# Cross-attention by units of eight heads: four key buffers, pairs of score tiles, values in runs, score maxima ahead across units

## What is computed

```python
q = (layernorm(x) @ w_q.T).reshape(8, 56, 16, 8)
k = (ctx @ w_k.T).reshape(8, 1500, 16, 8)
v = (ctx @ w_v.T).reshape(8, 1500, 16, 8)
attn = softmax(einsum('bqhd,bkhd->bhqk', q, k) * 8 ** -0.5, axis=-1)
x = x + tanh(g_xattn) * (einsum('bhqk,bkhd->bqhd', attn, v).reshape(8, 56, 128) @ w_o.T)
# then: layernorm, router softmax, top 2 of 8 experts (128 -> 2 x 512 -> 128, gelu gate)
x = x + tanh(g_ffn) * sum_over_top2(weight * expert(layernorm(x)))
```

## Time and profile before

| | us |
|---|---|
| median of 3 runs (332.04 to 336.74) | 333.3 |
| the profiled execution | 336.0 |
| its span, first to last instruction | 333.9 |
| prologue, up to the first scores of batch 0 | 42.67 |
| one batch in the steady loop | 25.18 |
| the last attend block of batch 7 starts at | 237.84 |
| from there to the end of the span | 96.1 |

### The profile page before, as it was taken

One profiled execution on the slowest core, in us unless ns is written; L12 is line 12 of the kernel. 1 busy time (PEld: TensorE's weight loads), 2 busy tenths in 40 slices (PEclk: granted clock), 3 DMA queues, 4 the chain that ended last, 5 costly groups with the idle time before them and its releaser, 6 DMA issues.

```text
span 333.9 us, 7738 instructions
## 1 busy us (share of the span) xinstructions
PE 298.5 (89%) x2761; PEld 216.6 (65%) x2761; DVE 228.7 (69%) x407; ACT 184.8 (55%) x360; POOL 93.2 (28%) x102
## 2 busy tenths in 40 slices
PE   0957589998999999999999999999568899999875
PEld 0444277676677677677677677777466688887653
DVE  4449957866857858858858858942234788888874
ACT  0612046665676676666666666548616477775422
POOL 6065001141141131131132130001331066664330
PEclk9979859999999999999999999999855999999979
DMA  6994921277197087097097095600000000000000
GB/s 173 112 249 115 226 77 39 47 159 254 25 211 236 13 198 251 8 201 253 6 196 260 0 201 162 202 2 2 2 0 0 2 0 0 0 0 1 1 0 27
DMA packets 14755, 32.67 MB, mean 98 GB/s; under 512 B 4416, under 2 KB 8128, under 8 KB 14736
## 3 DMA queue, kind: packets, MB, share of 16 engines
q1 hardware_dynamic: 13504, 32.09, 37.7%
q10 hardware_dynamic: 720, 0.27, 0.3%
q0 software_dynamic: 512, 0.07, 0.2%
HBM read 13.06 MB, written 0.23 MB: 40 GB/s over the span
## 4 chain that ended last, share of the span: by engine, by line
PE 66%; issue 12%; DVE 8%; POOL 4%; DMA 4%; SPq 3%; ACT 2%; DVEq 0%; POOLq 0%; ACTq 0%
PE score_ps L787 15%; PE o_ps L807 13%; PE max_ps L798 9%; PE misc_ps L777 5%; PE misc_ps L771 4%; DMA ctx_sb<-in_ctxT 4%; PE score_ps L969 3%; SPq L217 3%; PE score_ps L971 2%; PE score_ps L970 2%; POOL wo_sb L340 2%; DVE kx L738 2%; DVE probs L733 2%; DVE k_low L719 2%; PE o_ps L969 1%
## 5 line engine op out<-in xcount | busy, mean ns | idle before, releaser
L590 DVE TENSOR_REDUCE part_max<-max_ps 112x1 f32<-112x512 f32 (+1 forms) x192 | 119.8, 670 | 30.4 <-PE max_ps L798 29.4
L441 ACT ACTIVATE probs<-score_ps 128x448 f32<-128x448 f32 x192 | 94.6, 543 | 55.3 <-PE score_ps L787 54.8
L798 PE MATMUL max_ps<-kx,qx 96*112 96x512 f32 (+1 forms) x192 | 80.9, 440 | 3.3 <-DVE part_max L590 2.8
L787 PE MATMUL score_ps<-qx,kx 112*128 112x224 f32 (+1 forms) x384 | 78.5, 301 | 1.2 <-DVE qx L609 1.2
L787 PEld LDWEIGHTS score_ps<-qx,kx 112*128 112x128 f32 (+1 forms) x384 | 60.9, 190 | 19.3 <-issue 13.9
L807 PE MATMUL o_ps<-probs,v_sb 128*32 128x112 f32 (+1 forms) x1536 | 58.1, 266 | 0.4 <-ACT probs L441 0.4
L324 POOL TENSOR_TENSOR k_low<-k_full,k_high 128x512 fp32r<-128x512 f32 (+1 forms) x18 | 22.5, 1251 | 106.7 <-ACT k_full L427 106.7
L807 PEld LDWEIGHTS o_ps<-probs,v_sb 128*32 128x32 f32 (+1 forms) x1536 | 34.8, 109 | 25.1 <-ACT probs L441 11.4
L798 PEld LDWEIGHTS max_ps<-kx,qx 96*112 96x112 f32 x192 | 33.4, 181 | 12.6 <-issue 6.8
L367 POOL TENSOR_TENSOR kx<-gu_sb,kx 128x512 fp32r<-128x512 f32 x16 | 22.8, 1426 | 44.9 <-ACT kx L488 44.9
L522 ACT ACTIVATE kx<-probs 128x448 fp32r<-128x448 f32 x32 | 18.5, 577 | 23.0 <-DVE probs L733 22.2
(11 more groups left out here) (149 smaller groups left out, 374.5 us busy)
## 6 DMA issues: line engine op xcount, KB each, us to landing
kx<-k_high SPq DMA_DIRECT2D x64, 128.0 KB, 2.4
ctx_sb<-in_ctxT SPq DMA_DIRECT2D x7, 750.0 KB, 4.4
kx<-k_low SPq DMA_DIRECT2D x32, 128.0 KB, 2.4
gu_sb<-in_guT SPq DMA_DIRECT2D x8, 512.0 KB, 5.0
kx<-k_high SPq DMA_DIRECT2D x64, 59.5 KB, 2.8
dn_sb<-in_dnT SPq DMA_DIRECT2D x8, 256.0 KB, 5.6
kx<-k_low SPq DMA_DIRECT2D x32, 59.5 KB, 2.9
ctx_sb<-in_ctxT SPq DMA_DIRECT2D x2, 256.0 KB, 6.8
```

Of the source, the lines that this page charges most:

```text
L441: nc.scalar.activation(probs[0:m, t % 2, SC // 2 * h:SC // 2 * (h + 1)], score_ps[0:m, hs % NB, 0:SC // 2], ACT.Exp, scale=SCALE).then_inc ...
L590: nc.vector.reduce_max(part_max[:, p, c:c + 1], max_ps[0:PC, n % NB, 0:size], AX.X).then_inc(max_taken, 1)
L787: last = nc.tensor.matmul(score_ps[0:m, hs % NB, GC * (g % 2):GC * (g % 2) + GC], kx[0:KR, par, g, 128 * t:128 * t + m], qx[0:KR, par, g, ...
L798: nc.tensor.matmul(max_ps[0:PC, n % NB, 0:size], qx[0:MR, par, p // 2, PC * (p % 2):PC * (p % 2) + PC], kx[0:MR, par, p // 2, start:start ...
```

## The change

A batch is cut in two units of eight heads (`h` = 0, 1); 16 units in all. For each unit there is a key buffer of its own (four in all, of half the size: `kx` is as large as before), filled by 6 DMAs of whole rows (1500 keys), 12 a batch. The ones rows are 8 instead of 16.

- Scores: `scores` computes two key tiles of a unit (4 matmuls) into two of four banks; `exp_pair` is one activation of 2 x 448 columns. `probs` holds four such pairs.
- Values: `attend` is a run of 16 matmuls (four key tiles), three runs a unit, instead of 8 matmuls in each of 12 steps a batch.
- Maxima: 12 products a unit. During unit u PE does the last seven of unit u+1 and the first five of unit u+2. They, the transpose of the maxima and the denominators share one ring of two banks of `max_ps`: 14 turns a unit, each of which waits until the turn two before it has been read (`next_bank`).
- The copy of `o_ps` moves from DVE to ACT (`o_copy`), and the reciprocal is of 112 columns, twice a batch.
- Prologue: the queries and keys of the first unit are made first, only its 12 products (and five of the second unit) are done before the loop, the second unit's keys are moved by ACT's queue, the context of batch 1 is loaded before the key moves, the ones rows after them, and the low parts of batch 1's keys are made by POOL rather than DVE. A dummy Exp loads ACT's table before the first copy.
- End: the projections of tokens (`project_out`) stand between units 13 and 14, the transposes of their tokens in the last unit behind all its scores.

Engine PE, inside the loop before: one step `t` with its attend block (`score_ps`, `max_ps`, `o_ps` are PSUM tiles).

The core of the diff (the first `attention` is DVE's, the second PE's; constants: `HP` 4, `PAIRS` 6, `TRIOS` 3, `UM` 12, `RING` 14; `ring(u, k)` is the number of turn k of unit u):

```diff
-        kx = sb("kx", [128, 2, G, KPAD], f32r)
+        kx = sb("kx", [128, 4, 2, KPAD], f32r)
...
-        score_ps = pb("score_ps", [128, NB, 512])
-        max_ps = pb("max_ps", [128, NB, 512])
+        score_ps = pb("score_ps", [128, 4, 512])
+        max_ps = pb("max_ps", [128, 2, 512])
...
+            def move_unit(par, h):
+                for g in range(2):
+                    move_keys(sp, 2 * par + h, h, g, (0, TK), kx_loaded[2 * par + h][g])
...
+                sp.wait_ge(k_low_saved, NCH * (b + 3))
+                sp.wait_ge(scores_done, PAIRS * (2 * b + 1))
+                move_unit(par, 0)
+                sp.wait_ge(scores_done, PAIRS * (2 * b + 2))
+                move_unit(par, 1)
...
+            def exp_pair(i, par, h, k):
+
+                act.wait_ge(scores_done, PAIRS * unit(i, par, h) + k + 1)
+                slot, bank = (PAIRS * h + k) % 4, 2 * (k % 2)
+                nc.scalar.activation(probs[:, slot, :, :], score_ps[:, bank:bank + 2, 0:SC // 2],
                                      ACT.Exp, scale=SCALE).then_inc(exp_done, 1)
+            def o_copy(i, par, h):
+
+                u = unit(i, par, h)
+                act.wait_ge(o_norm_ready, u + 1)
+                act.wait_ge(pv_done, TRIOS * (u + 1))
+                nc.scalar.activation(o_sb[:, PC * h:PC * h + PC], o_ps[:, PC * h:PC * h + PC], ACT.Copy
+                                     ).then_inc(o_saved, 1)
...
+            def attention(i, par, h, after=True):
+
+                u = unit(i, par, h)
+                for n in range(5, UM):
+                    take_max(ring(u, n - 5), (n - 5) % 2, n)
+                negate_max(u + 1, ring(u, UM - 5))
+                if after:
+                    take_max(ring(u, 7), 1, 0)
+                turn = 8 if after else 7
+                max_rows(ring(u, turn), turn % 2, *ahead(i, par, h, 1)[1:])
+                if after:
+                    for n in range(1, 5):
+                        take_max(ring(u, 8 + n), n % 2, n)
+                turn = RING - 1 if after else 8
+                invert(i, par, h, ring(u, turn), turn % 2)
...
+            def next_bank(turn):
+
+                pe.wait_ge(max_taken, turn - 1)
...
+            def attention(i, par, h, jobs=True, job_next=True, after=True, middle=None):
...
+                scores_next(i, par, h, 1)
+                next_max(5)
+                scores_next(i, par, h, 2)
+                next_max(6)
+                if jobs:
+                    project(i, par, h, 1)
+                next_max(7)
+                scores_next(i, par, h, 3)
+                next_max(8)
+                attend(i, par, h, 0)
+                next_max(9)
+                scores_next(i, par, h, 4)
+                next_max(10)
+                attend(i, par, h, 1)
+                next_max(11)
+                scores_next(i, par, h, 5)
+                later_max(0)
+                if jobs:
+                    project(i, par, h, 2)
+                turn = 8 if after else 7
+                transpose_max(u + 1, ring(u, turn), turn % 2)
+                later_max(1)
+                attend(i, par, h, 2)
+                later_max(2)
+                pe.wait_ge(exp_done, PAIRS * u + PAIRS)
+                scores(*u1, 0, ring(u, turn) + 1)
+                later_max(3)
+                if job_next:
+                    project(*u1, 0)
+                later_max(4)
+                turn = RING - 1 if after else 8
+                denominators(i, par, h, ring(u, turn), turn % 2)
...
-            body(3, 0, keys_next=False)
-            body(3, 1, keys_next=False, next_batch=False)
+            attention(3, 0, 0, job_next=False)
+            attention(3, 0, 1, jobs=False, job_next=False)
...
+            project_out(0, NR - 1)
+            attention(3, 1, 0, jobs=False, job_next=False, after=False)
+            for k in range(1, PAIRS):
+                scores_next(3, 1, 1, k)
+                if k == 3:
+                    attend(3, 1, 1, 0)
+            pe.wait_ge(max_taken, ring(NU - 2, 9))
+            transpose_tokens(0, NR - 1, NR)
+            attend(3, 1, 1, 1)
+            attend(3, 1, 1, 2)
+            denominators(3, 1, 1, ring(NU - 2, 9), 1)
```

More of the change, by code:

```diff
@@ L189, in batch, with unit, ring, ahead @@
             return 2 * i + par
+        def unit(i, par, h):
+            return 4 * i + 2 * par + h
+        def ring(u, k):
+            return RING0 + RING * u + k
+        def ahead(i, par, h, k):
+            i1, par1 = nxt(i, par, (h + k) // 2)
+            return i1, par1, (h + k) % 2
         def counts(eng, *values):
@@ L264, in _ @@
             body(2, 1, ctx_next=False)
-            body(3, 0, ctx_next=False, keys_next=False)
-            for e in range(B - 1, E):
+            for e in range(B - 2, E):
                 load_expert(e)
```

635 lines of the change are left out of this document (331 added, 304 removed).

## The result

| | before | after |
|---|---|---|
| median of 12 runs each, us | 333.06 (332.04 to 337.69) | 335.68 (334.3 to 338.18) |
| ratio of the medians, 95% interval | | 1.007 [1.0039, 1.0101] |
| span of the profiled execution | 333.9 | 335.3 |
| first scores | 42.67 | 38.42 |
| one batch in the steady loop | 25.18 | 25.68 |

The change makes the kernel 0.4 to 1.0% slower. The prediction was 324.0 with a range of 312 to 335: wrong, and wrong in sign. The time is within 2% of before, to which the prediction had given 0.32. Both profiled executions are on the long side of their kernels (336.0 us before, 337.0 after), so their spans differ by 1.4 us where the medians differ by 2.6.

A forecast was written before the change was run, and what follows sets the result against it. PE's own sequence was taken to bound the loop, DVE's reductions the prologue. Gaining 11.2 us in the prologue, giving back 1.0 in the loop's end stages and 0.9 at the end made 9.3 less: 324.0 us, range 312 to 335.

The forecast's parts named there:

- To t = 0 of unit 0 ... 35.4: Prologue: first scores at 31.5 instead of 42.67, another 1.85 and 2.0 for half clock, so the first unit starts at 35.4.
- the walk: Step-by-step timing of prologue and one unit in PE's order: first scores 30.5 before a half-clock allowance, unit waits 0.95.
- rival 3: Prologue: late ones rows or the context hold first scores to 40, 8.5 of the gain goes; 332 to 333, chance 0.10.
- A unit is 12.57: Steady loop: one unit takes 12.57 us, 11.6 of work and 0.95 of waits; twelve units take 150.8.
- PE's bare sequence ... 11.6 a unit: Loop: PE's work without waits falls from about 24.9 to 23.2 us a batch, 11.6 a unit.
- transposes and denominators add 0.2 to 0.3: Loop: in the new order these two small PE operations cost 0.2 to 0.3 us more a batch.
- Unit 12 ... 11.7, unit 13 ... 10.9: Behind the loop: 0.9 less without the last projection; then 2.8 less work without any projections, but 1.15 more waits on DVE.
- Unit 14 and the last unit: Late units: 9.2 us with seven products, then the last run of values at 6.9 into the last unit, at 227.6.
- The end: Last run of values to output projection: about 5.2 us against 4.29, 0.9 lost, with two POOL splits ahead of the last normalisation.
- ACT off the path: Loop: ACT doesn't set the time; 896-column activations at 0.82 us give 8.7 us of its work in a 12.6 us unit.
- The clock: Loop: PE's waits at two max products a unit lower the clock; 340 to 350, say 344, chance 0.12.
- own signs: Prediction wrong if first scores come after 36, a unit differs by over 0.6 from 12.57, or the clock falls in the loop.

The follow-up runs named there:

- experiment 7: Changed kernel, but the second unit's six key moves are issued by SP, ahead of the ones rows, instead of by ACT: 336.26 us, ratio to before 1.0048.
- experiment 4: Changed kernel, but each unit's third run of values stands ahead of the max product that waits: 330.03 us, ratio to before 0.9904.
- experiment 5: Changed kernel, but each pair of score tiles is read by two exponentials of 448 columns instead of one of 896: 335.46 us, ratio to before 1.0069.
- experiment 11: Changed kernel, but POOL's last normalisation stands behind one of two weight subtractions instead of behind both: 335.65 us, ratio to before 1.0066.
- experiment 1: Changed kernel, but each DVE reduction of a max product reads only half of its columns: 325.75 us, ratio to before 0.9777.
- experiment 9: Against a kernel with three maxima banks, SP issuing the second unit's moves and an earlier last normalisation: SP's ones moves put before its first wait; 325.12 us.

## Why the prediction was wrong

The last run of values was forecast at 227.6 and came at 238.77, 11.2 us later. By the prediction's own steps (their sum, with roundings, is 11.2):

- **"To t = 0 of unit 0 ... 35.4": it was 41.11, 5.7 late.** The first products were right (17.1 against 16 to 17). Then ACT's six issues took 5.2 us for 3.6, the first value copy stood at 21.85 for 19.2, and product 3 at 24.21 for 20.8: 3.4 late. From there to the first scores the walk had 10.7 us, one of them for half clock, and it took 14.2: 3.5 more. Some 2.5 of these are the long stretch at half clock, as the kernels with the same prologue show (experiment 7), and 0.7 is DVE's cast beside POOL's work. Behind the first scores 1.2 of this came back. Experiment 7 shows that the walk of products and reductions itself was good: without ACT's issues the last product before the scores starts at 30.24, and the walk had the scores at 30.5. It also shows what the walk left out: a second chain, the ones rows. They landed at 33.70 in the changed kernel, where nothing waited for them, but 2.2 behind the forecast's first scores at 31.5, so that forecast would have failed on them even without ACT's issues. The text had their late issue as rival 3, and gave it 0.10. By the profiles of experiments 4, 5 and 11, up to 2.8 of the 5.7 vary from execution to execution.
- **"A unit is 12.57": it was 12.84, 12 units 3.5 late.** The waits were placed rightly (first and ninth product) and not too small: the bare unit of experiment 1 and the real one differ by 0.70, the walk had 0.95. The mis-sized term is "PE's bare sequence ... 11.6 a unit": it is 12.14, that is 24.28 a batch for 23.2.

  Added up from one start to the next over a batch, before (91.65 to 116.83) and in experiment 1, the 1.1 us come apart. The sum started from "about 24.9", where PE was busy for all of 25.18: 0.3. Values, scores and max products together went from 20.37 to 19.01, 1.4 less where 1.8 was forecast (the runs of values alone from 6.37 to 5.43; one costs 0.90): 0.4. Transposes went from 0.04 to 0.58, denominators from 0.23 to 0.28, and the projections gave 0.1 back, where "transposes and denominators add 0.2 to 0.3" stood: 0.2. And the prediction's own terms (24.9 less 1.8, plus 0.2 to 0.3) give 23.3 to 23.4, not 23.2: 0.1 to 0.2.

  The transposes are dearer because of where they stand. Before, they stand between values and take little: from 118.36 to the next block 0.02, from 118.47 0.03. Now the pair takes 0.29, and the product behind it 0.41 instead of 0.32, twice a batch. PE of experiment 1 shows both:

```profile
108.62 0.36 PE L928 MATMUL max_ps<-ident,neg_max_parts 112*8 112x112 f32 x2
108.91 0.48 PE L905 MATMUL max_ps<-kx,qx 96*112 96x512 f32 x1
109.32 0.98 PE L919 MATMUL o_ps<-probs,v_sb 128*32 128x112 f32 x32
```

- **"Unit 12 ... 11.7, unit 13 ... 10.9": 12.85 and 12.06, 2.3 late together.** Unit 12 lost 0.9 us of work in the forecast and 0.26 in the trace (PE busy 12.11 against 12.37 in an average steady unit), and its idle time grew by as much, from 0.47 to 0.74. For unit 13 the forecast had 2.8 us less work and 1.15 more of waits; PE is busy 1.8 us less (10.60) and idle 1.0 more. So the waits where the projections had been cover were sized rightly, and the work that falls away with the projections was put too high, as far as the modelled busy time tells.
- **Unit 14 and the last unit: right** (9.37 for 9.2; the last run 6.48 behind unit 15's start).
- **The end: right in direction, half in size** (4.75 against 4.29, 0.5 lost for the 0.9 forecast); experiment 11 shows that the reason was too narrow.
- **ACT off the path: right** (experiment 5). The exponential of 896 columns took 0.92 us for the 0.82 assumed.
- **The clock: right to be a rival.** The rule of the Trainium skill, page "TensorE: Matmul & The Clock Gate", section "A second HAM failure mode: psum-queue depth-cycling", would have made the loop lose. In the loop PE stood idle 0.94 us of 25.68 in waits of up to 0.6, and the granted clock was 1.00. Here the trace doesn't bear the rule out. Half clock appeared in the prologue, from 22.30 in a wait of 3 us and once more until 42.8, in the first unit, and then only behind the loop (0.50 from 244.16 to 257.82).

By its own signs the prediction failed at the first scores (38.42, with 36 as its limit), and not at the unit or the clock. The mechanism of the loop was seen, each wait at its place, and the sign still came out wrong. A forecast gain of 9.3 us stood on a prologue that was 5.7 short, by the price of ACT's issues and by half clock, and on a loop "taken as even", where 0.27 a unit over 12 units is a per cent of the time. The sum also books 11.2 us to the prologue, while by its own times t = 0 moves from 43.66 to 35.4 only, 8.3 us; the other 1.9 to 2.0 stand between there and the last run of values, where the kernel before had two long batches (27.28 and 26.31).

## What to carry to other kernels

When a ring of banks gets shorter, price each turn as producer, consumer and the small operations that stand ahead of the consumer, and put a long independent block of the producer's behind the tightest turn: here one moved run of values was worth 1.7% (experiment 4), and a third bank, taken from the scores, 2.2%. When a prologue is reordered, walk every chain that ends in its first scores, the last-issued transfer too; one that was hidden can set the new end. Compare prologues by several executions, since 2.5 us went here with the length of a stretch at half clock that the same code had or had not. Work that is removed from the bound engine gains less where it was also the cover for another engine: unit 13 had 1.8 us less of it and was 0.8 shorter.

## What the runs showed that was not expected

- DMA issues are not of one price: 0.58 us for the first key moves on ACT's queue, 1.43 for the fifth, and 3.35 for one on SP's queue behind the four moves of ones (experiment 9). The engine that issues stands still for that long.
- Taking away a wait of 4.6 us for the ones gave 0.15 us at the first scores (experiment 9): 2.4 were lost to a later first product and 1.6 to DVE's small operations.
- A cast of 112x4 values on DVE took 0.17 us, and 0.87 and 1.10 (experiment 4) while POOL's subtractions of 128x512 ran. The two long ones end within 0.04 us of the end of POOL's work (36.49 and 36.46, 33.13 and 33.09). That it is this work that delays them is inferred from the times, not tested.
- A third bank is worth 15 us in one order of the same work and 7 in the other (there it was taken from the scores).
